# Order of the second phase: the transposes of n3 one pair later, the CB product and the transposes of n2 later, n2 in a buffer of its own

## The reference

```python
def attn_ref(x):                      # L0_attn
    x = x + linear_attention(layernorm(x, ln1_g, ln1_b), wq, wk, wv, wo)
    h = layernorm(x, ln2_g, ln2_b)
    return x + lookup_act(h @ w1) @ w2        # 256 -> 1024 -> 256, gelu on a grid of step 0.1
def ffn_ref(x):                       # L0_ffn
    return einsum('bsk,nk->bsn', x, CB) * (SCB / 127.0) + bias
x = x + attn_ref(layernorm(x))
x = x + ffn_ref(layernorm(x))
```

## Time and profile before

| | |
|---|---|
| median of 3 runs | 652.83 us (643.82 to 653.84) |
| the profiled execution | 651.4 us, span of the core 649.6 us |
| granted TensorE clock, mean | 0.975 of full |
| PE busy, PEld busy | 586.2 us (90%), 517.6 us (80%) |
| DVE, ACT, POOL busy | 517.0 us (80%), 411.7 us (63%), 386.2 us (59%) |
| one chunk of phase 2 (i = 1 to 13) | about 27.3 us |

### The profile page before, as it was taken

One profiled execution on the slowest core, in us unless ns is written; L12 is line 12 of the kernel. 1 busy time (PEld: TensorE's weight loads), 2 busy tenths in 40 slices (PEclk: granted clock), 3 DMA queues, 4 the chain that ended last, 5 costly groups with the idle time before them and its releaser, 6 DMA issues.

```text
span 649.6 us, 12205 instructions
## 1 busy us (share of the span) xinstructions
PE 586.2 (90%) x3838; PEld 517.6 (80%) x3838; DVE 517.0 (80%) x1076; ACT 411.7 (63%) x767; POOL 386.2 (59%) x337
## 2 busy tenths in 40 slices
PE   6999999999997999898998989989899898998875
PEld 6887787878786878788787978879788797887675
DVE  5488988898873688878888788887988878888656
ACT  2377767676765685675756757576665766657560
POOL 3446475655542447676486765757657576675553
PEclk8599999999997999999999999999999999999898
DMA  8101112021101000000100001010110000100001
GB/s 287 53 34 65 59 38 65 32 65 34 66 1 36 17 32 33 32 32 32 65 32 32 33 33 65 32 32 32 32 65 32 32 32 32 65 24 11 33 1 67
DMA packets 11128, 29.16 MB, mean 45 GB/s; under 512 B 2016, under 2 KB 4576, under 8 KB 11104
## 3 DMA queue, kind: packets, MB, share of 16 engines
q1 hardware_dynamic: 9472, 28.32, 12.3%
q10 hardware_dynamic: 1632, 0.53, 0.4%
HBM read 20.45 MB, written 8.39 MB: 44 GB/s over the span
## 4 chain that ended last, share of the span: by engine, by line
PE 36%; DVE 27%; issue 16%; POOL 12%; ACT 6%; DMA 1%; DVEq 1%; ACTq 0%; POOLq 0%; SPq 0%
PE psum L914 31%; DVE f_arena L729 8%; POOL f_arena L355 5%; DVE bn_stats L615 5%; PE psum L932 4%; POOL rstd L324 3%; DVE f_arena L755 3%; DVE f_arena L657 2%; DVE mean_var L622 2%; ACT grid_index L540 2%; DVE f32r_arena L738 2%; POOL pow_arg L322 2%; ACT f32r_arena L550 2%; ACT f32r_arena L494 1%; DVE f_arena L642 1%
## 5 line engine op out<-in xcount | busy, mean ns | idle before, releaser
L914 PE MATMUL psum<-w_hi,f32r_arena 128*128 128x256 f32 x1280 | 178.7, 286 | 5.1 <-DVE f32r_arena L738 3.5
L914 PEld LDWEIGHTS psum<-w_hi,f32r_arena 128*128 128x128 f32 x1280 | 164.9, 190 | 16.0 <-issue 11.5
L914 PE MATMUL psum<-f32r_arena,w_hi 128*128 128x512 f32 x512 | 143.0, 411 | 3.7 <-issue 3.7
L540 ACT ACTIVATE grid_index<-psum,w_bias_in_steps 128x512 int8<-128x512 f32 x128 | 87.2, 681 | 69.9 <-PE psum L914 69.9
L729 DVE TENSOR_SCALAR f_arena<-f_arena,mean_var,rstd 128x256 f32<-128x256 f32 x124 | 102.7, 887 | 25.9 <-POOL rstd L324 25.9
L914 PE MATMUL psum<-f32r_arena 128*128 128x512 f32 (+1 forms) x512 | 120.5, 378 | 2.6 <-issue 1.5
L343 POOL TENSOR_TENSOR f32r_arena<-f_arena,f32r_arena 128x512 fp32r<-128x512 f32 x64 | 86.0, 1344 | 56.3 <-ACT f32r_arena L550 56.3
L914 PEld LDWEIGHTS psum<-f32r_arena,w_hi 128*128 128x128 f32 x512 | 91.1, 194 | 22.4 <-ACT grid_index L540 4.7
L932 PE MATMUL psum<-ident,f_arena 128*128 128x128 f32 x504 | 69.6, 283 | 36.9 <-DVE f_arena L729 32.3
L932 PEld LDWEIGHTS psum<-ident,f_arena 128*128 128x128 f32 x504 | 58.6, 145 | 52.1 <-issue 28.3
L914 PEld LDWEIGHTS psum<-f32r_arena 128*128 128x128 f32 x512 | 83.2, 190 | 14.9 <-issue 3.1
(11 more groups left out here) (96 smaller groups left out, 976.4 us busy)
## 6 DMA issues: line engine op xcount, KB each, us to landing
f_arena<-in_L_attn_x_dram SPq DMA_DIRECT2D x32, 512.0 KB, 3.3
out_dram<-f_arena SPq DMA_DIRECT2D x15, 512.0 KB, 2.6
f_arena<-in_L_attn_w_dram SPq DMA_DIRECT2D x2, 1024.0 KB, 11.3
out_dram<-f_arena SPq DMA_DIRECT2D x2, 256.0 KB, 2.2
phi_q<-in_L_attn_wk_dram ACTq DMA_DIRECT2D x1, 256.0 KB, 4.9
phi_q<-in_L_attn_wv_dram ACTq DMA_DIRECT2D x1, 256.0 KB, 5.4
phi_q<-in_L_attn_wq_dram SPq DMA_DIRECT2D x1, 256.0 KB, 5.7
phi_q<-in_L_ffn_CB_dram SPq DMA_DIRECT2D x1, 256.0 KB, 7.8
```

The costliest lines, as they stand in the source:

```text
L540: act(k8[:, m % 2], bank(AB + m % 2), ACT.Identity, scale=1.0 / STEP, bias=h_bias[:, m:m + 1]).then_inc(s["grid_ready"], 1)
L914: return nc.tensor.matmul(out_, lhs, rhs, start=start, stop=stop, skip_group_check=True)
```

## The change

- PE: one more pair (down 2, up 5) goes ahead of the transposes of n3. down 4 goes ahead of the CB product (it stood behind the transposes of n2 and up 7). Behind CB come up 7, attention half 0, and only then the transposes of n2.
- ACT: gelu 4 goes ahead of high of n3, and quantise 5 too; quantise 7 goes ahead of high_h.
- DVE: norm2 goes ahead of low of n3, mlp_low 5 ahead of ot, attend half 0 ahead of low_h.
- n2 has a buffer of its own, n2t. POOL and SP are unchanged.

```diff
--- before.py
+++ after.py
@@ -135,7 +135,7 @@
 
         take = carve(f_arena)
         x2 = [take(CE) for _ in range(2)]
-        take(CE)
+        n2t = take(CE)
         xz, xp, xb, ot = (take(CE) for _ in range(4))
         tf = [take(CHUNK) for _ in range(2)]
         scb_b, bias_b = take(D), take(D)
@@ -568,19 +568,20 @@
                 if nn:
                     copy_phi(i + 2)
                 if main:
-                    quantise(i, 4)
+                    mlp(i, 4)
+                    quantise(i, 5)
                 if prv:
 
                     a.wait_ge(s["o_done"], o_before_c)
                     high(i - 1, "n3_turned", SA, "s_hi_c")
                 if main:
-                    gelu(i, 4)
-                    mlp(i, 5)
+                    gelu(i, 5)
                     mlp(i, 6)
+                    quantise(i, 7)
                 if nxt:
                     high_h(i + 1)
                 if main:
-                    mlp(i, 7)
+                    gelu(i, 7)
 
             body(0, False, True, True, True, 0)
             with a.Fori(1, CHUNKS - 2) as i:
@@ -723,10 +724,10 @@
                                      ALU.mult).then_inc(s["attn_tile"], 1)
 
 
-            def normalise(c, src, mv, r, powered, done):
+            def normalise(c, src, dst, mv, r, powered, done):
                 v.wait_ge(s[powered], c + 1)
                 for j in range(TT):
-                    i = ve.tensor_scalar(tm(nt)[:, j], tm(src)[:, j], mv[:, 2 * j:2 * j + 1], r[:, j:j + 1],
+                    i = ve.tensor_scalar(tm(dst)[:, j], tm(src)[:, j], mv[:, 2 * j:2 * j + 1], r[:, j:j + 1],
                                          ALU.subtract, ALU.mult)
                 i.then_inc(s[done], 1)
 
@@ -758,7 +759,7 @@
 
             def norm2(c):
                 v.wait_ge(s["mv2_ready"], c + 1)
-                normalise(c, y2, mv2, r2, "pow2", "n2_ready")
+                normalise(c, y2, n2t, mv2, r2, "pow2", "n2_ready")
 
             def low_h(c):
 
@@ -787,26 +788,25 @@
                 if prv:
 
                     v.wait_ge(s["mv3_ready"], i)
-                    normalise(i - 1, xp, mv3, r3, "pow3", "n3_ready")
+                    normalise(i - 1, xp, nt, mv3, r3, "pow3", "n3_ready")
                 if main:
                     mlp_low(i, 3)
                 if nxt:
                     first_residual(i + 1)
+                    norm2(i + 1)
                 if prv:
                     low(i - 1, SA, "s_hi_c", "s_lo_c")
-                if nxt:
-                    norm2(i + 1)
+                if main:
+                    mlp_low(i, 5)
                 if prv:
                     v.wait_ge(s["cb_done"], i + 2)
                     wait(v, s["out_ready"], i)
                     ve.tensor_tensor(tm(ot), two(SA).rearrange("p (j d) -> p j d", j=TT),
                                      scb_b.unsqueeze(1).to_broadcast([P, TT, D]), ALU.mult).then_inc(s["ot_ready"], 1)
-                if main:
-                    mlp_low(i, 5)
+                if nn:
+                    attend(i + 2, 0)
                 if nxt:
                     low_h(i + 1)
-                if nn:
-                    attend(i + 2, 0)
                 if main:
                     mlp_low(i, 7)
                 if nn:
@@ -1094,7 +1094,7 @@
             def turn2(c):
                 pe.wait_ge(s["n2_ready"], c + 1)
                 pe.wait_ge(s["y2_ready"], c + 1)
-                turn(nt, of_chunk(c, SB2, AB), "n2_turned")
+                turn(n2t, of_chunk(c, SB2, AB), "n2_turned")
 
             def phase2(exact):
                 def weight_terms(hi, lo, wh, wl):
@@ -1145,34 +1145,25 @@
                     if main:
                         down(i, 1)
                         up(i, 4)
+                        down(i, 2)
+                        up(i, 5)
                     if prv:
                         pe.wait_ge(s["n3_ready"], i)
                         pe.wait_ge(s["attn_tile"], attended)
                         turn(nt, SA, "n3_turned")
                     if main:
-                        down(i, 2)
-                        up(i, 5)
                         down(i, 3)
                         up(i, 6)
+                        down(i, 4)
                     if prv:
                         pe.wait_ge(s["s_hi_c"], i * KT)
                         pe.wait_ge(s["s_lo_c"], i * KT)
                         rows(SA, s_hi, s_lo, cbh, cbl, not exact).then_inc(s["cb_done"], 1)
-                    if nxt and prv:
+                    up(i, 7)
+                    if attend_seq is not None:
+                        attention(i + 2, attend_seq, 0)
+                    if nxt:
                         turn2(i + 1)
-                        up(i, 7)
-                        down(i, 4)
-                        if attend_seq is not None:
-                            attention(i + 2, attend_seq, 0)
-                    elif nxt:
-
-                        attention(i + 2, attend_seq, 0)
-                        up(i, 7)
-                        turn2(i + 1)
-                        down(i, 4)
-                    else:
-                        up(i, 7)
-                        down(i, 4)
                     down(i, 5)
                     down(i, 6)
                     if attend_seq is not None:
```

## The result

The changed kernel takes 717.33 us, the median of 4 runs (714.34 to 722.16); the kernel before, run beside it, took 651.58 us. The ratio is 1.106, 95% interval 1.100 to 1.112: it is slower by 10.6%, 66 us. The profiled execution has a span of 718.5 us (before 649.6) and a mean granted clock of 0.929 (before 0.975).

The account below looks back on a forecast made before the run. A loop through all the engines, 27.28 us a chunk, was taken as the bound. 651.4 us profiled plus 46.8 for waits, 1.0 for chunks 0, 14 and 15 and 9.1 for the clock gave 708.3, stated as 708; range 686 to 724.

Parts of the forecast that it names:

- the band 703 to 722: Whole kernel: the predicted waits plus a clock fall in some or most chunks, 0.35 to 1.7 us a chunk; 50%.
- The chain up to n2's statistics does not change.: DVE and POOL: no moved instruction lies on this chain, so n2's normalisation still starts 17.3 us behind up 0.
- down 2 waits for mlp_low 2: PE ahead of down 2: a new wait of 0.9 us for POOL's mlp_low 2.
- down 4 waits for mlp_low 4 behind the power: PE ahead of down 4: waits 2.5 us, since POOL makes its t_lo only behind the power for n2.
- CB waits for low of n3 behind n2's normalisation: PE ahead of the CB product: another 1.4 us of waiting for DVE's low half of n3.
- ot and mlp_low 7: PE: waits of 0.7 us for ot ahead of attention half 0 and 0.75 us for mlp_low 7 ahead of down 7.
- The waits make 3.6 us a chunk.: Chunks alike: period 30.9 us against 27.3, with PE waiting 6.2 us in place of 2.06.
- Rival 1: PE's waits vanish: period 25.2 us, PE's own work, and 623 us in all; 3%.
- The clock, 0.7 us a chunk.: PE behind the gap at down 4: granted clock falls, costing 0 to 1.7 us a chunk, taken as 0.7.
- Chunks 0, 14 and 15: Chunks unlike the rest: +0.5 us for chunk 0, +1.0 for 14, -0.5 for 15, together 1.0 us.
- Rival 4: DVE's mlp_low 7 meets POOL's last addition: up to 1.44 us a collision, 19 us more, 727 us; 8%.

Follow-up runs that it names:

- both gates open: Changed kernel with POOL's mlp_low 4 ahead of n2's power and DVE's low of n3 ahead of n2's normalisation: 661.32 us; with POOL's last addition held back, 645.59 us.
- the two runs with one gate open: Changed kernel with either POOL's mlp_low 4 ahead of n2's power, 705.87 us, or DVE's low of n3 ahead of n2's normalisation, 693.57 us.
- the run with three edits and POOL's last addition held back: Kernel before with n3's transposes one pair later, down 4 ahead of CB, mlp_low 4 ahead of n2's power, POOL's last addition after mlp_low 7: 636.72 us.
- the run with the gate on DVE open: Changed kernel with DVE's low of n3 ahead of n2's normalisation again: 693.57 us (1.070).

## Why the prediction was right, and where it was off

The prediction was 708 us in a range of 686 to 724, slower with 94%; measured 717, in the upper half of the band 703 to 722 that had 50%. The mechanism was right, the size of one term was not. The predicted waits count from the moment at which PE is free by the pace of starts. The waits in brackets count from the modelled end of a matmul and are, with the clock up, 0.15 to 0.2 us smaller, so both measures are given. Step by step:

- *The chain up to n2's statistics does not change.* Right: n2's normalisation at 17.36 us behind up 0, before 17.35.
- *down 2 waits for mlp_low 2:* 0.9 us predicted; 0.83 by the starts, 0.68 in brackets.
- *down 4 waits for mlp_low 4 behind the power:* 2.5 us predicted; 2.5 by the starts (407.19 - 403.74 - 0.94), 2.33 to 2.36 in brackets. That POOL's order is the cause is shown by the run that changed it alone.
- *CB waits for low of n3 behind n2's normalisation:* 1.4 us predicted; 1.4 by the starts (409.60 - 407.19 - 1.02), in brackets 0.92 in the chunk shown and 1.36 in every other one (with the clock low, down 4 itself ends later and eats some of it). Shown by the run that changed DVE's order alone.
- *ot and mlp_low 7:* 0.7 and 0.75 us predicted. Where the clock stayed up, 0.64 and 0.74 by the starts, 0.47 and 0.48 in brackets; in the changed kernel ot's wait is 0.38 or nothing, since the slow up 7 covers it.
- *The waits make 3.6 us a chunk.* With the clock held up a chunk took 30.8 to 31.0 us, predicted 30.9: the term is right to 0.1 us, and not by luck, as each wait is right to 0.1 us too. One comparison in the prediction is of unlike measures, though: "6.2 in place of 2.06" sets waits by the starts against waits in brackets. By the starts the kernel before waits 2.6 us (1.7 for n3, 0.2 ahead of CB, 0.65 for n2), and 6.2 less 2.6 is the 3.6. Rival 1's 25.2 us a chunk rests on the 2.06 and is 0.5 us too high by the same measure.
- *The clock, 0.7 us a chunk.* This is the term that was mis-sized: it is 1.5 us (32.4 - 30.9). From one fall behind two gaps I made one fall in two chunks. The windows show a fall in each of the thirteen chunks, in turn a short one (377.2 to 380.6) and one of twice the length (407.9 to 414.8). I had also let much of the slow stretch pass in the wait ahead of CB. In fact the long one began within down 4, and the short one just ahead of CB's first matmul; each covered all of CB, or nearly.
- *The error of the sum.* The profiled execution took 720.25 us, 12 more than the 708.3 worked out for it: 13 x 0.8 = 10 us are the clock, 2 us the next term. The median of the runs lies 3 us below the profiled execution, where I had put it at the same level; that the error is 9 us and not 12 is luck.
- *Chunks 0, 14 and 15:* +1.0 us predicted, 3.0 measured (0.2 + 2.8); the parts were not told apart further. In chunk 14 down 4 waits 2.63 us and the clock falls as in the others.
- *Rival 4*, mlp_low 7 meeting POOL's addition, did not occur in the changed kernel (0.69 us; 2.2 us lay between the two where the prediction left 0.7), but in four of the experiments, in one of them at mlp_low 5. For this kernel the low chance was borne out, and the mechanism decided how four of the experiments came out.
- *Rival 1*, the waits vanish, was refused for the right reason. The two runs with both gates open say more: even then this order gives 28.4 us a chunk, and 27.3 with the collision out of the way too.

## What to carry to other kernels

When work is moved forward on the engine that is the bound, look up for each moved piece who makes its input and what stands ahead of that producer in its own order: here one unmoved line on POOL turned a moved matmul into a wait for another chain. A gap that a move opens costs more than its length when the clock falls with it (here 3.6 us a chunk and 1.5 us on top), and two gates in a row must be opened together. And two engines whose instructions hold each other up can be kept apart by a wait on the one with time to spare: it took 32, 17 and 16 us off three of the orders here, and without it none of them was more than 1% faster than the kernel before.

## What the runs showed of the hardware

The waits here are those in brackets. In the changed kernel and in the two runs with one gate open, each chunk alike has a wait of 2.3 us or of 3.3 to 3.4 us, and the granted clock fell in all of these chunks but one: within the wait, within about a microsecond behind it, or in the next wait. Behind waits of 1.76 us it fell in five chunks of thirteen. In the runs in which no wait of a chunk was over 1.6 us it stayed up, but for two chunks of the run with the nine matmuls, where it fell at waits of 1.37 and 1.20 us. The length of the wait alone does not decide: the single one of 2.48 us in the kernel before had no fall behind it, nor had one of 2.72 us near the end of the run with three edits and POOL's last addition held back. In the chunks alike a slow stretch lasted 3.4 or 6.8 us, and always 3.4 us in the run with the gate on DVE open, where no second gap followed. Nine matmuls without use in the gap kept the clock up in eleven chunks of thirteen and made the kernel 18 us faster.

An mlp_low on DVE (two inputs in SBUF) that began while a POOL addition ran ended 0.55 us behind the end of that addition in the chunk read of each of the four runs with the collision, and took 1.81, 2.09, 2.59 and 2.62 us in place of 0.68; PE's wait for it was up to 1.78 us. n3's normalisation, which reads one tensor in SBUF and two scalars per partition, was held up as well: 4.34 us beside xz and then mlp_low 2, 2.35 us beside mlp_low 2 alone; n2's took 2.25 us beside mlp_low 4 and 1.80 us without it. The Trainium skill's page "GPSIMD Engine Reference" (section "Key points") states that the two engines share their SBUF interfaces and contend when a VectorE instruction is in a 2-port perf mode or has two SBUF inputs. For mlp_low, which has two SBUF inputs, the runs agree, with the times above; whether the normalisation runs in such a mode no run here shows.
